# Layer 3's self-attention in one pass with three score buffers and shared output banks, and its cross-attention with plain head values

## The chip, the cores and the metric

One core of a Trainium2 chip runs the whole program. The metric is device time in microseconds of one execution, as the median of several. A profiled execution is longer by its profiler's share and is given beside its span, the time from its first to its last instruction.

## The reference

Four layers act on x (2 x 1024 tokens of 256 features) with a context of 2 x 64 tokens of 128 features. Each layer adds a gated attention part and a gated feed-forward part. The change touches layer 3's attention part only:

```
def mha(x, y, ..., causal):                 # H = 16 heads of D = 32
    q, k, v = ln(x) @ wq, ln(y) @ wk, ln(y) @ wv
    a = softmax(q @ k.T * D ** -0.5)        # over all keys
    if causal: a = a * (key > query)        # after the softmax: later keys only
    x_out = x + (a @ v, heads side by side) @ li1_w + li1_b
    return x_out + gelu(ln(x_out) @ li2_w + li2_b) @ li3_w + li3_b
x = ln(xx); x = x + mha(x, x, ..., causal=True)      # self-attention, 1024 keys
x = ln(x);  out = x + mha(x, ee, ..., causal=False)  # cross-attention, 64 keys
```

The softmax of the self-attention runs over all 1024 keys, but only keys after the query keep their weight. So a tile of 128 queries needs all its scores for the sum, and only the chunks of keys from its own on for the output.

## The kernel before

The program is a row of stages with a barrier between them. In each, every engine has its own list of instructions, written out by loops in Python, and engines wait for each other on semaphores that count. SP issues the DMAs, PE multiplies, ACT takes exponentials and copies, DVE reduces and copies, POOL multiplies and masks. PSUM has 8 banks of 512 fp32 columns.

`stage_self_project` normalises, multiplies by wq, wk and wv for pairs of 256 tokens, splits queries and keys into three bf16 parts and sends them to scratch in HBM, one entry for each batch and group of four heads (ENTRIES = 8). For the first batch it also sends the first group once more, as entry 8, a dummy. After the fourth pair SP waits until all that was sent has landed and loads entry 0 (`load_entry`: 16 DMAs of 256 KB and one of 512 KB), and then goes on with the sends of the next pairs. ACT waits for the sends of pair k-2 before it reuses their buffers (L2139).

`stage_self_attention` runs the entries in a hardware loop of two passes with a body of four entries (BODY = 4). After each pass the semaphores are cleared behind a barrier. An entry has 8 query tiles in the order 0, 7, 1, 6, 2, 5, 3, 4, and each tile four heads: 32 units. A block is one tile's four units; it has KC - si chunks of keys to turn and multiply, so 8, 1, 7, 2, 6, 3, 5, 4 in that order. In step v of the loop over units:

- PE computes the scores of unit v into one of two buffers of two banks (banks 0 to 3), once the exponentials of unit v-2 are taken. Then it transposes the masked probabilities of unit v-5 (`turn`), in groups of up to 4 chunks, into banks 4 and 5 in turn. From step 10 on it also does a quarter of the output product of a finished block (`output(w, q)`), into banks 6 and 7 in turn, one or two chunks at a time.
- DVE takes the row maxima of unit v (L2390), copies its share of the groups of unit v-5 (`store_turned`, side 1, L2361) and inverts the sum of unit v-1 (L2397).
- ACT copies its share (side 0), takes the exponentials of unit v with their sum (L2373), and every fourth step copies a finished output (L708).
- POOL multiplies by the inverse and masks.

Before an output begins, PE waits until the groups of that block are copied. They were transposed in the step before or earlier.

`stage_attention` serves layers 0, 2 and 3. It folds the keys into Wq, so that scores come straight from the features. For wider heads the values are folded into Wo as well (`fold_v`), and a tile's output is 8 products of 128 x 256. With `narrow`, which holds for layer 2 only (16 columns a head), the values stay as they are: the products of the probabilities with the head values go to bank 7, ACT copies them (`heads`, L708), and their product with Wo is the output. The norm's transposes use bank 7 too, so PE waits for that copy ahead of them, at every second tile.

Of the kernel before, what the change touches and what calls it, by code (L numbers as in the profile page):

```python
# [5 lines left out]
F32 = mybir.dt.float32  # L6
I32 = mybir.dt.int32
BF16 = mybir.dt.bfloat16
ALU = mybir.AluOpType
# [326 lines left out]
def stage_attention(core, a, name, width, scale, plan, following, source, out_tile, gate, bias,  # L336
# [16 lines left out]
    narrow = width * 4 <= KEYS  # L353
# [1617 lines left out]
def self_attention_scratch(nc):  # L1971


    def dram(name, shape, dtype):
        return nc.dram_tensor(name, shape, dtype, kind="Internal").ap()


    parts = [[dram(f"l3_{kind}_part{m}", [ENTRIES + 1, P, TOK], BF16) for m in range(3)] for kind in ("q", "k")]
    values = dram("l3_values", [ENTRIES + 1, P, KC, P], F32)
    heads_out = dram("l3_heads_out", [ENTRIES, P, TOK], F32)  # L1980
    return parts, values, heads_out
# [46 lines left out]
def stage_self_project(core, a, x1, scratch, entry, plan):  # L2028
# [6 lines left out]
    with ExitStack() as ctx:  # L2035
# [21 lines left out]
        with nc.Block() as block:  # L2057
            @block.sync
            def _(sp):
                total = [0, 0]  # L2060
                for k in range(PAIRS):
                    b, p, at = k // (PAIRS // B), k % 2, (k % (PAIRS // B)) * PAIR
                    places = [(b * GROUPS, GROUPS)]
                    if b == 0:
                        places.append((ENTRIES, 1))
# [23 lines left out]
            def sent_before(k):  # L2089

                return sum(16 * 8 * (2 if q < PAIRS // B else 1) for q in range(k % 2, k, 2))
# [104 lines left out]
def stage_self_attention(core, scratch, entry, following):  # L2196
# [8 lines left out]
    BODY = 4  # L2205
# [20 lines left out]
    assert BANKFULS % 2 == 0  # L2226

    def groups_through(u):

        return sum(1 for g in groups if g[0] <= u)  # L2230

    with ExitStack() as ctx:
# [13 lines left out]
        with nc.Fori(0, ENTRIES // BODY) as jj:  # L2246
            sem, clear_semaphores = named_semaphores(nc, "l3s")
            scores_ready, measured, exped, inverted = sem("scores_ready"), sem("measured"), sem("exped"), sem("inverted")
            masked, turned, stored = sem("masked"), sem("turned"), [sem("stored0"), sem("stored1")]
            out_ready, out_stored = sem("out_ready"), sem("out_stored")  # L2250
            out_sent = [sem(f"out_sent{e}") for e in range(BODY)]

            with nc.Block() as block:
                @block.sync
                def _(sp):
                    load_entry(sp, scratch, entry, BODY * jj + 1, 1)
                    for e in range(BODY):

                        sp.wait_ge(out_ready, KC * (e + 1))
                        if e < BODY - 1:  # L2260
                            load_entry(sp, scratch, entry, BODY * jj + e + 2, e % 2)
                        sp.wait_ge(out_stored, KC * (e + 1))
                        sp.dma_start(out_scratch[bass.ds(BODY * jj + e, 1)].rearrange("a p n -> p (a n)"),
                                     heads_out[:, e % 2, :]).then_inc(out_sent[e], 16)
                    for e in range(BODY):
                        sp.wait_ge(out_sent[e], 16)

                @block.gpsimd
                def _(pool):
                    for v in range(BODY * UNITS):  # L2270
                        si = tile_of(v)
                        pool.wait_ge(inverted, v + 1)
                        nc.gpsimd.tensor_tensor(ex[v % RING][:, si * P:], ex[v % RING][:, si * P:],  # L2273
                                                sm[:, v % RING:v % RING + 1].to_broadcast([P, TOK - si * P]), ALU.mult)
                        pool.drain()
                        nc.gpsimd.affine_select(out=ex[v % RING][:, si * P:(si + 1) * P], in_=ex[v % RING][:, si * P:(si + 1) * P],
                                                compare_op=ALU.is_gt, fill=0.0, base=0, pattern=[[1, P]],
                                                channel_multiplier=-1).then_inc(masked, 1)

                @block.tensor  # L2280
                def _(pe):
                    def ends_at(si):

                        return max(range(si, KC), key=lambda c: ((c - si) % R, c))

                    def scores(v):
                        p, si, r = v // UNITS % 2, tile_of(v), v % R
                        if v >= 2:
                            pe.wait_ge(exped, v - 1)
                        for h in range(2):  # L2290
                            for s in range(2):
                                last = nc.tensor.matmul(ps[:, 2 * (v % 2) + h, :],  # L2292
                                                        stack[p][0][s][:, r, si * P:(si + 1) * P],
                                                        stack[p][1][s][:, r, h * 512:(h + 1) * 512],
                                                        start=(s == 0), stop=(s == 1))
                        last.then_inc(scores_ready, 1)

                    def turn(v):
                        e, si = v // UNITS, tile_of(v)
                        pe.wait_ge(masked, v + 1)  # L2300
                        for g, (u, c0, size) in enumerate(groups):
                            if u != v % UNITS:
                                continue
# [424 lines left out]
```

## Time and profile before

| | us |
|---|---|
| median of 3 runs (2522.53 to 2523.38) | 2523.2 |
| the profiled execution | 2524.31 |
| its span | 2522.6 |
| PE busy | 2047.2 (81%) |
| DVE busy | 1367.6 (54%) |
| ACT busy | 929.6 (37%) |
| POOL busy | 710.5 (28%) |

The mean granted clock of TensorE is 0.902 of full speed. Busy shares are means over stages that differ: in the experts' stages PE is nearly alone, in the self-attention (about 969 to 1477 us) four engines work at once. So the stages are read one by one, from a table of stretches and from timelines.

### The profile page before, as it was taken

The numbers are of one execution on the slowest core, as the hardware profiler recorded it, in microseconds if no ns is written. First come the engines' busy times: TensorE is split into PE (matmuls) and PEld (weight loads), VectorE is DVE, ScalarE is ACT, GpSimd is POOL, SyncE is SP. The second block draws the span as 40 slices with busy tenths as digits, with TensorE's granted clock in tenths as the row PEclk, the third lists the DMA queues.
The fourth block names the chain that finished last, engine by engine and source line by source line (L and its number), as shares of the span: only waits on it lengthen the run. The fifth ranks groups of instructions, "written<-read, shape, count | busy, mean of one in ns | idle before, by whom it ended". The sixth has DMA issues, their size and how long they took to land. (4 is left out here: it accounts for less than half of the span.)

```text
span 2522.6 us, 36317 instructions
## 1 busy us (share of the span) xinstructions
PE 2047.2 (81%) x11904; PEld 1504.7 (60%) x11904; DVE 1367.6 (54%) x3511; ACT 929.6 (37%) x1859; POOL 710.5 (28%) x1199
## 2 busy tenths in 40 slices
PE   5983974467867677999799979969898589999991
PEld 4661863354444454555455558846687378888991
DVE  4871006535745765888688847757636432222332
ACT  4220321112324346888688843232232112222230
POOL 0223011030130125777577751102330230000005
PEclk9995995578979789999999989979999699999995
DMA  2004531000011286333333430110000525555684
GB/s 87 1 1 150 167 104 28 13 13 14 1 19 12 82 216 165 85 85 85 86 65 92 97 108 11 28 36 1 1 13 1 193 104 175 175 175 175 215 287 115
DMA packets 171504, 219.20 MB, mean 87 GB/s; under 512 B 39911, under 2 KB 133540, under 8 KB 165184
## 3 DMA queue, kind: packets, MB, share of 16 engines
q1 hardware_dynamic: 163344, 196.65, 26.7%
q0 software_dynamic: 7264, 20.31, 2.5%
q8 instruction: 88, 1.44, 0.2%
q14 instruction: 88, 0.72, 0.1%
q10 hardware_dynamic: 720, 0.07, 0.0%
HBM read 171.13 MB, written 46.14 MB: 86 GB/s over the span
## 5 line engine op out<-in xcount | busy, mean ns | idle before, releaser
L2390 DVE TENSOR_REDUCE l3s_mx<-banks 128x1 f32<-128x1024 f32 x256 | 313.1, 1223 | 96.7 <-PE banks L2292 93.8
L2292 PE MATMUL banks<-l_stack 128*128 128x512 bf16 x1024 | 268.1, 385 | 44.1 <-ACT xn_tokens L2373 21.0
L1012 PE MATMUL banks<-l3f_xrt,l3f_w 128*128 128x256 f32 (+1 forms) x1536 | 277.9, 342 | 2.7 <-issue 1.5
L1012 PEld LDWEIGHTS banks<-l3f_xrt,l3f_w 128*128 128x128 f32 x1536 | 249.6, 192 | 29.1 <-issue 3.3
L1302 DVE TENSOR_SCALAR l3f_sg<-banks 128x256 f32<-128x256 f32 (+1 forms) x192 | 72.0, 375 | 287.5 <-PE banks L1012 287.5
L2273 POOL TENSOR_TENSOR xn_tokens<-xn_tokens,l3s_sm 128x1024 f32<-128x1024 f32 (+3 forms) x128 | 201.6, 1575 | 50.3 <-DVE l3s_sm L2397 49.2
L222 PE MATMUL banks<-ident,xn_tokens 128*128 128x128 f32 x320 | 64.7, 338 | 166.8 <-DVE xn_tokens L211 148.0
L2292 PEld LDWEIGHTS banks<-l_stack 128*128 128x128 bf16 x1024 | 80.8, 98 | 163.3 <-ACT xn_tokens L2373 52.6
L2373 ACT ACTIVATE xn_tokens<-banks,l3s_mx 128x1024 f32<-128x1024 f32 x128 | 142.7, 1115 | 46.2 <-DVE l3s_mx L2390 45.1
L222 PEld LDWEIGHTS banks<-ident,xn_tokens 128*128 128x128 f32 x320 | 46.6, 172 | 188.4 <-DVE xn_tokens L211 133.0
L2373 ACT ACTIVATE x_features<-banks,l3s_mx 128x1024 f32<-128x1024 f32 x128 | 143.0, 1117 | 27.9 <-DVE l3s_mx L2390 27.6
L1077 ACT ACTIVATE l3f_sg<-l3f_sg 128x256 f32<-128x256 f32 (+1 forms) x192 | 72.2, 376 | 208.9 <-DVE l3f_sg L1302 208.9
L1025 PE MATMUL banks<-l3f_w,l3f_ht 128*128 128x256 f32 x624 | 138.5, 379 | 0.0
L930 POOL DMA_DIRECT2D l3f_results<-l3f_yt x24 | 15.8, 658 | 410.7 <-ACT l3f_yt L708 410.7
L1025 PEld LDWEIGHTS banks<-l3f_w,l3f_ht 128*128 128x128 f32 x624 | 116.8, 190 | 14.9
L2537 PE MATMUL banks<-x_features,weights 128*128 128x256 f32 x512 | 117.5, 390 | 4.3 <-ACT x_features L235 2.4
L2308 PEld LDWEIGHTS banks<-ident,xn_tokens 128*128 128x128 f32 x832 | 96.5, 140 | 29.1 <-issue 10.2
L2550 PE MATMUL banks<-weights,l3m_ht 128*128 128x256 f32 x512 | 113.2, 379 | 0.4 <-DVE l_x L2605 0.4
L2308 PE MATMUL banks<-ident,xn_tokens 128*128 128x128 f32 x832 | 112.6, 273 | 0.5 <-ACT l3s_pt L2359 0.5
L2537 PEld LDWEIGHTS banks<-x_features,weights 128*128 128x128 f32 x512 | 100.1, 196 | 19.5 <-issue 3.8
L2273 POOL TENSOR_TENSOR x_features<-x_features,l3s_sm 128x128 f32<-128x128 f32 (+3 forms) x128 | 92.4, 722 | 65.6 <-DVE l3s_sm L2397 64.6
L2359 ACT ACTIVATE l3s_pt<-banks 128x384 f32<-128x384 f32 (+2 forms) x192 | 97.0, 505 | 24.2 <-PE banks L2326 18.5
(532 smaller groups left out, 3925.4 us busy)
## 6 DMA issues: line engine op xcount, KB each, us to landing
l3f_w<-in_L_ffn_gate_up_w_dram SPq DMA_DIRECT2D x24, 2048.0 KB, 7.6
l3f_w<-in_L_ffn_down_w_dram SPq DMA_DIRECT2D x24, 1024.0 KB, 6.0
l_stack<-l_q_part SPq DMA_DIRECT2D x72, 256.0 KB, 6.0
l_stack<-l_k_part SPq DMA_DIRECT2D x72, 256.0 KB, 11.4
l0f_w<-in_L_ffn_W_dram SPq DMA_DIRECT2D x16, 1024.0 KB, 5.8
l_q_part<-l_stack SPq DMA_DIRECT2D x24, 256.0 KB, 3.0
l_k_part<-l_stack SPq DMA_DIRECT2D x24, 256.0 KB, 3.7
l3f_rows<-l3f_zero SPq DMA_DIRECT2D x13, 384.0 KB, 4.1
```

The costliest lines, as they stand in the source:

```text
L222: last = nc.tensor.transpose(ps[:, bank, c * PAIR + u * P:c * PAIR + (u + 1) * P], src(2 * j + u)[:, c * P:(c + 1) * P], core["ident"][:, :])
L1012: last = nc.tensor.matmul(ps[:, f % 4, h * PAIR:h * PAIR + size], w1_sb[:, p, dc, h * FF + f * P:h * FF + (f + 1) * P], xrt[:, p, dc, 0:si ...
L1025: last = nc.tensor.matmul(ps[:, 4 + p, u * D:(u + 1) * D], ht[:, p, f, u * P:(u + 1) * P], w2_sb[:, p, f, :], start=(f == 0), stop=(f == F ...
L1077: nc.scalar.activation(sg[:, f % 4, 0:size], sg[:, f % 4, 0:size], ACT.Silu).then_inc(silued, 1)
L2273: nc.gpsimd.tensor_tensor(ex[v % RING][:, si * P:], ex[v % RING][:, si * P:], sm[:, v % RING:v % RING + 1].to_broadcast([P, TOK - si * P]) ...
L2292: last = nc.tensor.matmul(ps[:, 2 * (v % 2) + h, :], stack[p][0][s][:, r, si * P:(si + 1) * P], stack[p][1][s][:, r, h * 512:(h + 1) * 512 ...
L2308: last = nc.tensor.transpose(ps[:, 4 + n % 2, c * P:(c + 1) * P], ex[v % RING][:, (si + c0 + c) * P:(si + c0 + c + 1) * P], core["ident"][ ...
L2359: last = op.activation(dst, src, ACT.Copy)
L2373: nc.scalar.activation(ex[v % RING][:, :], ps[:, 2 * (v % 2):2 * (v % 2) + 2, :].rearrange("p a n -> p (a n)"), ACT.Exp, bias=mx[:, v % RI ...
L2390: nc.vector.tensor_reduce(mx[:, v % RING:v % RING + 1], ps[:, 2 * (v % 2):2 * (v % 2) + 2, :].rearrange("p a n -> p (a n)"), AX_X, ALU.max ...
L2537: last = nc.tensor.matmul(ps[:, n % 4, 0:PAIR], w2[:, dc, f * P:(f + 1) * P], core["xt"][:, dc, PAIR * j:PAIR * (j + 1)], start=(dc == 0), ...
L2550: last = nc.tensor.matmul(ps[:, 4 + k % ring, u * D:(u + 1) * D], ht[:, k % 2, f, u * P:(u + 1) * P], w3[:, f, :], start=(f == 0), stop=(f ...
```

## The change

- Self-attention: the hardware loop goes; all 256 units are written out in one pass. There are three score buffers (banks 0 to 5), and scores wait for the exponentials of v-3. Turned probabilities and outputs share banks 6 and 7 in turn, in one running count of uses (`uses`), by whose parity ACT (even) or DVE (odd) copies them out. The output of a block is done at once, at one step in four, right after that step's transposes, and waits until every use before it is copied out on both sides. ACT and DVE copy an output at the start of their next step (`store_output`).
- The dummy entry goes, in scratch, in the projection's sends and as a load at the end.
- Cross-attention: `narrow` now holds for heads of 32 columns too, so layer 3's takes layer 2's path.

```diff
-    narrow = width * 4 <= KEYS
+    narrow = width * 2 <= KEYS
...
-                    if b == 0:
-                        places.append((ENTRIES, 1))
...
-    BODY = 4
+    SCORES = 3
+    uses = {}
+    for v in range(ENTRIES * UNITS + OUT):
+        if TURN <= v < ENTRIES * UNITS + TURN:
+            for g, group in enumerate(groups):
+                if group[0] == (v - TURN) % UNITS:
+                    uses["turn", (v - TURN) // UNITS, g] = len(uses)
+        if v >= OUT and (v - OUT) % R == 0:
+            uses["out", (v - OUT) // R] = len(uses)
+    def stored_through(side, n):
+        return (n + 2 - side) // 2
...
+                    if v >= SCORES:
+                        pe.wait_ge(exped, v - SCORES + 1)
...
+                        n = uses["turn", e, g]
+                        if n >= 2:
+                            pe.wait_ge(stored[n % 2], stored_through(n % 2, n - 2))
...
+                def output(w):
+                    e, si = w // KC, ORDER[w % KC]
+                    n = uses["out", w]
+                    for side in range(2):
+                        pe.wait_ge(stored[side], stored_through(side, n - 1))
+                    for c in range(si, KC):
+                        for r in range(R):
+                            last = nc.tensor.matmul(ps[r * W:(r + 1) * W, 6 + n % 2, 0:P], ...
+                    last.then_inc(out_ready, 1)
+                for v in range(ENTRIES * UNITS + OUT):
...
+                    if v < ENTRIES * UNITS:
+                        scores(v)
+                    if TURN <= v < ENTRIES * UNITS + TURN:
+                        turn(v - TURN)
+                    if v >= OUT and (v - OUT) % R == 0:
+                        output((v - OUT) // R)
...
+            def store_output(eng, op, v, side):
+                if v < OUT or (v - OUT) % R != 0:
+                    return
+                w = (v - OUT) // R
+                if uses["out", w] % 2 != side:
+                    return
+                eng.wait_ge(out_ready, w + 1)
...
+            @block.vector
+            def _(dve):
+                for v in range(ENTRIES * UNITS + OUT + 1):
+                    store_output(dve, nc.vector, v - 1, 1)
+                    if v < ENTRIES * UNITS:
+                        dve.wait_ge(scores_ready, v + 1)
+                        nc.vector.tensor_reduce(mx[:, v % RING:v % RING + 1], ...
+                    if v >= STORE:
+                        store_turned(dve, nc.vector, v - STORE, 1)
+                    if 1 <= v <= ENTRIES * UNITS:
+                        dve.wait_ge(exped, v)
+                        nc.vector.reciprocal(...).then_inc(inverted, 1)
...
-        nc.sync.wait_ge(loaded[0], 16 * LOADS * (ENTRIES // 2 + 1))
-        nc.all_engine_barrier()
```

## Rows read from the trace of the kernel before

**Rows 1.** Lines by shape, 940 to 1480 us: busy, mean ns, idle before.

```profile
L2390 DVE TENSOR_REDUCE l3s_mx<-banks 128x1 f32<-128x1024 f32 x256 | 313.1, 1223 | 96.7 <-PE banks L2292 93.8
...
L2361 DVE COPY l3s_pt<-banks 128x512 f32<-128x512 f32 x48 | 32.8, 682 | 6.3 <-PE banks L2308 5.7
...
L2361 DVE COPY l3s_pt<-banks 128x256 f32<-128x256 f32 x48 | 19.9, 415 | 0.9 <-PE banks L2308 0.9
```

**Rows 2.** Stretches: length; busy (count) of PE, PEld, DVE, ACT, POOL; PEclk, DMA, GB/s.

```profile
1089.29:1150.42 61.13, 58.92 (x562) 33.55 (x561) 51.91 (x88) 49.73 (x97) 45.74 (x65) 1.00 0.39 88
...
1209.68:1227.83 18.15, 8.90 (x119) 5.28 (x118) 3.59 (x8) 5.77 (x12) 3.82 (x6) 0.85 0.29 79
...
601.20:747.00 145.80, 114.08 (x608) 65.08 (x608) 100.12 (x145) 41.12 (x56) 23.58 (x112) 0.86 0.00 1
```

**Rows 3.** Timeline of units: start, length, engine, line, operation [idle before, releaser].

```profile
1089.29 1.23 DVE L2390 TENSOR_REDUCE l3s_mx<-banks 128x1 f32<-128x1024 f32 x1 [0.25 <-PE banks L2292]
...
1089.73 0.42 PE L2326 MATMUL banks<-l3s_pt,l_values_in 128*32 128x128 f32 x8
...
1090.09 1.04 PE L2292 MATMUL banks<-l_stack 128*128 128x512 bf16 x4
...
1090.43 0.41 DVE L2361 COPY l3s_pt<-banks 128x256 f32<-128x256 f32 x1
...
1090.96 0.60 PE L2308 MATMUL banks<-ident,x_features 128*128 128x128 f32 x4
...
1091.16 1.23 DVE L2390 TENSOR_REDUCE l3s_mx<-banks 128x1 f32<-128x1024 f32 x1 [0.24 <-PE banks L2292]
...
1093.21 0.64 PE L2326 MATMUL banks<-l3s_pt,l_values_in 128*32 128x128 f32 x16
...
1093.79 1.04 PE L2292 MATMUL banks<-l_stack 128*128 128x512 bf16 x4
```

**Rows 4.** Timeline: a copy on DVE and the weight load that waited for it.

```profile
1210.83 0.41 DVE L2361 COPY l3s_pt<-banks 128x256 f32<-128x256 f32 x1
...
1211.29 0.20 PEld L2308 LDWEIGHTS banks<-ident,xn_tokens 128*128 128x128 f32 x2 [0.21 <-DVE l3s_pt L2361]
```

**Rows 5.** Timeline: first and last reduction; a score group early in the second body.

```profile
968.92 1.22 DVE L2390 TENSOR_REDUCE l3s_mx<-banks 128x1 f32<-128x1024 f32 x1 [14.43 <-PE banks L2292]
...
1230.34 1.04 PE L2292 MATMUL banks<-l_stack 128*128 128x512 bf16 x4 [0.85 <-ACT xn_tokens L2373]
...
1468.58 1.23 DVE L2390 TENSOR_REDUCE l3s_mx<-banks 128x1 f32<-128x1024 f32 x1 [0.25 <-PE banks L2292]
```

**Rows 6.** Timeline of the projection: SP's issues and ACT's wait.

```profile
910.36 2.25 SPq L2078 DMA_DIRECT2D l_values<-l3p_vs  x4
...
914.27 1.78 SPq L2023 DMA_DIRECT2D l_stack<-l_q_part  x4
...
942.92 1.09 ACT L2139 ACTIVATE l_stack<-banks 128x512 bf16<-128x512 f32 x2 [9.00 <-DMA l_values<-l3p_vs]
```

**Rows 7.** Timeline of layer 3's cross-attention: folds, reductions, output.

```profile
1682.12 1.03 PE L482 MATMUL banks<-weights,l3a_blk 128*128 128x256 f32 x4
...
1773.58 1.22 DVE L631 TENSOR_REDUCE l3a_mx<-banks 128x16 f32<-128x1024 f32 x1 [0.98 <-PE banks L499]
...
1774.25 3.62 PE L542 MATMUL banks<-l3a_fold_v,l3a_pt 128*128 128x256 f32 x16
...
1781.78 1.23 DVE L631 TENSOR_REDUCE l3a_mx<-banks 128x16 f32<-128x1024 f32 x1 [1.11 <-PE banks L499]
```

**Rows 8.** Timeline of layer 2's cross-attention: scores, reduction, copy, transposes.

```profile
708.42 3.60 PE L499 MATMUL banks<-l2a_fold_q,x_features 128*128 128x512 f32 x8
...
712.35 1.21 DVE L631 TENSOR_REDUCE l2a_mx<-banks 128x16 f32<-128x1024 f32 x1
...
716.76 0.38 ACT L708 ACTIVATE l2a_heads<-banks 128x256 f32<-128x256 f32 x1
...
717.19 0.98 PE L222 MATMUL banks<-ident,xn_tokens 128*128 128x128 f32 x4 [2.66 <-ACT l2a_heads L708]
```

More of the change, by code:

```diff
@@ L1975, in dram @@
         return nc.dram_tensor(name, shape, dtype, kind="Internal").ap()
-    parts = [[dram(f"l3_{kind}_part{m}", [ENTRIES + 1, P, TOK], BF16) for m in range(3)] for kind in ("q", "k")]
-    values = dram("l3_values", [ENTRIES + 1, P, KC, P], F32)
+    parts = [[dram(f"l3_{kind}_part{m}", [ENTRIES, P, TOK], BF16) for m in range(3)] for kind in ("q", "k")]
+    values = dram("l3_values", [ENTRIES, P, KC, P], F32)
     heads_out = dram("l3_heads_out", [ENTRIES, P, TOK], F32)
@@ L2089, in sent_before @@
             def sent_before(k):
-                return sum(16 * 8 * (2 if q < PAIRS // B else 1) for q in range(k % 2, k, 2))
+                return sum(16 * 8 for q in range(k % 2, k, 2))
             @block.gpsimd
@@ L2349, in store_turned @@
                     for g, (u, c0, size) in enumerate(groups):
[L2350 to L2351 removed]
+                        if u != v % UNITS:
                             continue
[L2353 to L2357 removed]
@@ new lines, in turn @@
+                        last.then_inc(turned, 1)
+                def output(w):
+                    e, si = w // KC, ORDER[w % KC]
+                    n = uses["out", w]
+                    for side in range(2):
+                        pe.wait_ge(stored[side], stored_through(side, n - 1))
+                    for c in range(si, KC):
+                        for r in range(R):
+                            last = nc.tensor.matmul(ps[r * W:(r + 1) * W, 6 + n % 2, 0:P],
+                                                    values[:, e % 2, c, r * W:(r + 1) * W],
+                                                    pt[:, w % 2, r, c - si, :], start=(c == si),
+                                                    stop=(c == KC - 1))
+                    last.then_inc(out_ready, 1)
@@ new lines, in store_turned @@
+            def store_turned(eng, op, v, side):
+                if v >= ENTRIES * UNITS:
+                    return
+                e, w = v // UNITS, v // R
+                for g, (u, c0, size) in enumerate(groups):
+                    if u != v % UNITS or uses["turn", e, g] % 2 != side:
+                        continue
+                    n = BANKFULS * e + g
+                    eng.wait_ge(turned, n + 1)
+                    if w >= 2:
+                        eng.wait_ge(out_ready, w - 1)
+                    dst = pt[:, w % 2, v % R, c0:c0 + size, :].rearrange("p c n -> p (c n)")
+                    src = ps[:, 6 + side, 0:size * P]
+                    if side == 0:
+                        last = op.activation(dst, src, ACT.Copy)
+                    else:
+                        last = op.tensor_copy(dst, src)
+                    last.then_inc(stored[side], 1)
```

218 lines of the change are left out of this document (78 added, 140 removed).

## The prediction

> **What bounds the kernel now.** I read the page's slices first: the self-attention of layer 3 is the long even stretch from about 969 to 1477 us, a fifth of the span. The table of stretches then gives one entry (32 units of one tile and head) in its steady state: 61.13 us, in which PE is busy 58.92 and DVE 51.91 [rows 2]. So PE sets this stage, with DVE 9.2 us per entry behind it. The groups by line say the same: before the row maxima DVE stood idle 96.7 us, nearly all of it for PE's scores [rows 1]. Last I read the timeline of single units for the order on each engine, because the change is one of order. One step on PE: four score matmuls, 0.87 us until the transposes begin (1090.09 to 1090.96); the transposes, 0.11 us each plus 0.09 between parts; a piece of the output, 0.36 us for 8 records and 0.58 for 16, so 0.22 us per 8 records and about 0.13 fixed [rows 3]. On DVE: reduction, 1.14 us later the copy of turned probabilities, then the reciprocal [rows 3].
>
> From first to last reduction the stage takes 1468.58 - 968.92 = 499.7 us [rows 5]. That is 8 x 61.13 = 489.0, less one interval (1.9), plus the boundary between the two loop bodies, 18.15 where a step has 1.87 [rows 2], so 16.3; the sum, 503.4, is 3.8 too long, because the first entry of each body runs 1.9 faster (nothing to turn yet).
>
> **Self-attention, the boundary.** With one pass the drain and refill go: -16.3, and the second quick start with them: +1.9. Together -14.4 us. What is late next is the ordinary step.
>
> **Self-attention, the third score buffer.** Scores of unit v wait for the exponentials of v-3, not v-2. PE is busy 58.92 of 61.13 already, so this alone can give at most 2.2 us per entry. It also lets DVE work at its own rate wherever PE is ahead.
>
> **Self-attention, the outputs.** Before, the output of a block of four units goes in up to four pieces and waits for copies of transposes made at least one step earlier. Now turned probabilities and outputs share banks 6 and 7 in one running count n, and output n waits until everything up to n-1 is copied out on both sides. But n-1 is the group that PE transposed in this same step. I wrote the count out over one entry: in every block the second unit has a group on side 1, DVE's, whatever the block's length (for blocks of 1 to 4 chunks it is the only one, for 5 to 8 the first of two). DVE copies that group after the reduction of unit v. So once in four units PE must stand until DVE has finished the reduction of the newest scores and the copy; and no further scores can be issued meanwhile, since the output is ahead of them in PE's queue. Behind it wait scores v+1, on them DVE and ACT. The three buffers are empty at this point, by the order of the code.
>
> The hole that this leaves on DVE, from the end of the copy: 0.05 us to PE (copy ends 1211.24, PE's next load 1211.29 [rows 4]; I take 0.06), the output 0.13 + 0.22 m for m chunks, 1.07 from the scores' start to the reduction's [rows 3], less 0.15 for the reciprocal that fits in. That is 1.12 + 0.22 m. An entry has 8 outputs with m = 1 to 8, sum 36: 9.0 + 7.9 = 16.9 us. The output copies on DVE's side fall into the hole and cost nothing; without the hole they would be 4 x 0.28.
>
> DVE's own work: 51.9 us per entry. The sides change: of 24 copies per entry, two of 256 columns (415 ns) become two of 512 (682 ns) [rows 1], +0.5. So DVE's chain is 52.4 + 16.9 = 69.3 us per entry. Between outputs PE must keep up: for 8 chunks turned its step is 0.87 + 0.09 + 0.88 = 1.84, DVE's 1.14 + 0.60 + 0.12 = 1.86; equal, for short blocks PE is clearly quicker. Only for blocks of 5 and 7 does PE lag by 0.1 now and then; I add 0.3. Result 69.6 where 61.13 stood, though PE's own work falls (18 of the 26 pieces' fixed 0.13 go, 2.3 us).
>
> Bounds: if only PE's path counted (output, three steps, scores, reduction, copy) it would be 5.3 us fixed per output plus 0.22 m, 0.22 or 0.11 per turned chunk and the copy, 66.7 in all; if each of the 32 steps also lost 0.1 to a reciprocal or to POOL's queue, 73.
>
> In all: 8 x 69.6 = 556.8; the first entry lacks two outputs (4.2) and is 1.9 quicker; one interval less, 2.2: 548.5. Against 499.7: +48.8 us (with the bounds, +26 to +76). POOL (45.7 of 61.1 before) and ACT (49.7) stay below DVE. Drain and end of the stage stay as they are, within 1 us.
>
> **Projection.** The fifth copy of entry 0 goes: 8 DMA issues in each of the first four pairs, and the load of the dummy entry at the end. SP's issues take 2.25 us for 4 [rows 6], so 8 take 4.5. They sit right ahead of the wait for all sends, after which entry 0 is loaded (914.27). That load's 4.6 MB then hold up the sends, for which ACT waits 9 us until 942.92 [rows 6]. All of it moves up 4.5 us: -4.5 (none if the sends' bytes set it anyway, to -7 with 2 MB less to move). POOL's queue is not in it.
>
> **Cross-attention of layer 3.** It goes over to the path that layer 2 uses. Folds: 16 of 32 go, two records each of about 0.215 us at full clock, -6.9, and half the key/value products, about -0.9 [rows 7]; added are two value products of 512 columns (two records of 0.43 each, as in layer 2's scores [rows 8]), their mask on DVE (0.7, taken as a copy of 512 columns) and a handover: about -5.3. In the loop PE sets the time: 8.20 us from reduction to reduction with the norm's transposes, 7.76 without their four (0.44) [rows 7]. Of that 16 records of fold_v take 3.4; new are 8 records into Wo (1.8 with gaps) and 16 of 64-column weights. The latter no row shows. With 32 columns, four side by side, 8 records take 0.22 [rows 3], with 128 one takes 0.11: 16 records lie between 0.44 and 1.76. I take 0.88, half the array each, plus 0.14. A plain step becomes 7.24. At a norm step PE must now wait for ACT's copy of the head values, behind exp and the copy of the probabilities: in layer 2 that copy starts 4.41 us after the reduction and PE idles 2.66 for it, until 4.84 [rows 8]. Here it is 512 wide (0.6): transposes at 5.06, 0.5 for them, 3.44 scores, 0.2: 9.2 instead of 8.2. Twelve intervals: 95.4 before; 5.5 + 7 x 7.24 + 4 x 9.2 = 93.0 after, -2.4. The first of the twelve (5.5) is bound by DVE. The tail has one step more and its last outputs stand in the chain, twice at half clock: +3.5 to +5 by my estimate from the same records. Sum: -3 (from -6 to +12, if 64-column weights do not run side by side).
> By the page "TensorEngine Tiling (Array Packing)" of the Trainium skill (When to Use Tiling), weights of 64 columns give a column tiling of 2x; that is my 0.88. The trace before shows it for 32 columns only.
>
> **Sum.** +48.8 - 4.5 - 3 = +41. The profiled execution took 2524.31 us (span 2522.6), the median of the three is 2523.2; on the median: 2564.
>
> **The rivals.**
> *The output's wait is no more than the idle time DVE had* (faster). DVE idled 9.2 us per entry already; a third buffer can take that away. If the hole were 1.15 us per output instead of 2.1, an entry would stay at 61.1, and the rest decides: -14.4 - 4.5 - 3 = -22, 2501; with the waits met throughout, PE's work alone, about 58.5 per entry, 2480. It decides from 1.15 + 22/64 = 1.5 us per output. For it: PE's busy share; against it: output and scores alone are 1.07 + 0.13 + 0.22 m.
> *PE's clock falls* (slower still). In layer 2 a wait of 2.66 us is followed by matmuls at 1.2 GHz, and that stretch has a mean granted clock of 0.86; self-attention has 1.00 [rows 2, 8]. Here PE would wait 1.2 to 1.9 us per output. At half clock scores (0.87) and output (1.0) take about twice as long, 1.9 us more; at every second output that is 32 x 1.9, +60: 2625. In the first steps of a loop body PE waits 0.85 us of every 1.8 [rows 5] and the clock rises all the same, so I hold it unlikely.
> The Trainium skill ("TensorE: Matmul & The Clock Gate", A second HAM failure mode: psum-queue depth-cycling) says that short idle spells between groups, from cycling through PSUM banks, can make the clock swing and cost throughput; by it this rival would be the case.
> *Cross-attention's 64-column products run one after another*: 15 x 0.88, +13: 2577.
>
> **How the numbers follow.** Forecast 70% (own range 2540 to 2590), clock 10%, unpaired products 8%, the outputs' wait hidden 10% (of it 1 in 5 ends near no change), others 2%. Eight in ten: 2532 to 2594. Less than 0.2% (5 us) can't be told from no change. Faster 0.08, same 0.03, slower 0.89.
>
> **What would show it.** DVE's idle time before the reduction rises from 96.7 to some 140 us though the boundary is gone; before each output PE waits about 1.5 us, released by DVE's copy of turned probabilities; an entry takes 69 to 70 us; one gap of 18 us is missing; reductions in cross-attention 7.2 and 9.2 us apart. Wrong it is if outputs start less than 0.5 us after the transposes of their step, or if an entry stays below 62 us.

## The result, and the profile after

| | median us | runs | ratio to the kernel before (95%) |
|---|---|---|---|
| before | 2522.86 | 2519.68 to 2523.38 | |
| changed | 2558.07 | 2555.05 to 2561.02 | 1.0142 (1.0125 to 1.0160) |

The change makes the kernel 1.4% slower: 35 us, where the prediction had 41. The profiled execution took 2560.1 us, its span is 2558.5, so 35.9 more than the span before.

First the groups by line of the self-attention, 940 to 1520 us of the changed kernel (line, engine, operation, output<-input, shapes, count; busy us, mean ns; idle time of the engine before them, and what released it). They answer to [rows 1].

```profile
L2396 DVE TENSOR_REDUCE l3s_mx<-banks 128x1 f32<-128x1024 f32 x256 | 309.1, 1210 | 120.9 <-PE banks L2297 120.8
...
L2325 PE MATMUL banks<-l3s_pt,l_values_in 128*32 128x128 f32 x2304 | 76.2, 274 | 78.6 <-DVE l3s_pt L2359 72.9 <-ACT l3s_pt L2357 5.7
L2325 PEld LDWEIGHTS banks<-l3s_pt,l_values_in 128*32 128x32 f32 x2304 | 60.8, 109 | 92.9 <-issue 58.8 <-ACT l3s_pt L2357 34.0
...
L2359 DVE COPY l3s_pt<-banks 128x512 f32<-128x512 f32 x64 | 43.6, 681 | 3.5 <-PE banks L2313 3.5
...
L2374 DVE COPY weights<-banks 128x128 f32<-128x128 f32 x32 | 9.3, 291 | 28.8 <-PE banks L2325 28.8
```

DVE stood idle 120.9 us before the row maxima, where it was 96.7, though the 16 us of the boundary are gone. Almost all of it is a wait for PE's scores. PE in turn waited 72.9 us at the outputs (L2325) for DVE's copies of turned probabilities (L2359): 56 of the 64 waits. The other eight, one per entry, end with ACT's copy (5.7 us). Of the idle time of PEld, the weight load of the same outputs, 34.0 us end with ACT's copies (L2357). Before its copies of outputs (L2374) DVE stood another 28.8 us. The copy of 512 columns grew from 48 to 64 instances, as worked out.

One entry in the table of stretches, with the columns of [rows 2]:

```profile
1098.99:1167.55 68.56, 54.88 (x554) 35.73 (x560) 51.35 (x94) 48.51 (x93) 45.44 (x64) 1.00 0.34 78
```

The entry went from 61.13 to 68.56 us. PE was the full engine with 58.92 of 61.13; now it is busy 54.88 of 68.56 and no engine is full. When a stage gets longer while every engine in it gets emptier, a wait has taken over. The granted clock stays 1.00.

How it looks at one output, in the timeline of the changed kernel (start, length, engine, line, operation, [idle before, releaser]):

```profile
1118.66 1.21 DVE L2396 TENSOR_REDUCE l3s_mx<-banks 128x1 f32<-128x1024 f32 x1
...
1119.31 0.27 PE L2313 MATMUL banks<-ident,x_features 128*128 128x128 f32 x1
...
1119.78 0.15 DVE L2403 RECIPROCAL l3s_sm<-l3s_sm 128x1 f32<-128x1 f32 x1
1119.85 1.21 DVE L2396 TENSOR_REDUCE l3s_mx<-banks 128x1 f32<-128x1024 f32 x1
...
1120.97 0.28 DVE L2359 COPY l3s_pt<-banks 128x128 f32<-128x128 f32 x1
...
1121.40 1.95 PE L2325 MATMUL banks<-l3s_pt,l_values_in 128*32 128x128 f32 x64 [1.82 <-DVE l3s_pt L2359]
...
1123.51 0.81 PE L2297 MATMUL banks<-l_stack 128*128 128x512 bf16 x3 [0.16 <-issue]
...
1124.36 1.23 DVE L2396 TENSOR_REDUCE l3s_mx<-banks 128x1 f32<-128x1024 f32 x1 [3.04 <-PE banks L2297]
```

This is the output of an eight-chunk block; the group turned in its step has one chunk. DVE reduces the newest scores from 1119.85. PE put the one-chunk transpose into the queue ahead of the output, and it is long done. Its copy begins on DVE only at 1120.97, as the reduction ends. PE starts the output at 1121.40, having waited 1.82 us; the scores behind it start at 1123.51; DVE's next reduction comes at 1124.36, after 3.04 us of nothing to do. From the one reduction to the next it is 4.51 us where a step without an output takes 1.2 to 1.8.

First and last reduction of the stage (answers to [rows 5]):

```profile
967.22 1.23 DVE L2396 TENSOR_REDUCE l3s_mx<-banks 128x1 f32<-128x1024 f32 x1 [14.31 <-PE banks L2297]
...
1508.82 1.23 DVE L2396 TENSOR_REDUCE l3s_mx<-banks 128x1 f32<-128x1024 f32 x1 [0.66 <-PE banks L2297]
```

1508.82 - 967.22 = 541.6 us, 41.9 more than before, and no gap of 18 us stands between entries 4 and 5.

For the projection I take the two activation table loads that enclose it, of the kernel before and then of the changed one:

```profile
749.56 1.28 ACT L1938 ACT_TABLE_LOAD   x1
...
966.72 1.28 ACT L2373 ACT_TABLE_LOAD   x1 [10.58 <-PEq L44]
```

```profile
751.75 1.28 ACT L1938 ACT_TABLE_LOAD   x1
...
965.27 1.28 ACT L2387 ACT_TABLE_LOAD   x1 [10.73 <-PEq L44]
```

217.16 us became 213.52. Last, layer 3's cross-attention after the change: start of the stage, the first reduction, a step with the norm's transposes and the plain step behind it, and the last output of the tail (answers to [rows 7, 8]):

```profile
1701.10 0.10 POOL L424 MEMSET l3a_mask<- 128x4 f32 x1 [37.97 <-POOLq L44]
...
1722.18 1.22 DVE L631 TENSOR_REDUCE l3a_mx<-banks 128x16 f32<-128x1024 f32 x1 [3.79 <-PE banks L499]
...
1763.68 1.22 DVE L631 TENSOR_REDUCE l3a_mx<-banks 128x16 f32<-128x1024 f32 x1
...
1764.45 1.09 PE L522 MATMUL banks<-l3a_pt,l3a_v_blk 128*64 128x128 f32 x16
...
1765.47 1.99 PE L533 MATMUL banks<-weights,l3a_heads 128*128 128x256 f32 x8
...
1768.11 0.59 ACT L708 ACTIVATE l3a_heads<-banks 128x512 f32<-128x512 f32 x1
...
1768.75 0.66 PE L222 MATMUL banks<-ident,xn_tokens 128*128 128x128 f32 x4 [1.28 <-ACT l3a_heads L708]
...
1772.88 1.22 DVE L631 TENSOR_REDUCE l3a_mx<-banks 128x16 f32<-128x1024 f32 x1 [2.42 <-PE banks L499]
...
1780.13 1.22 DVE L631 TENSOR_REDUCE l3a_mx<-banks 128x16 f32<-128x1024 f32 x1 [1.00 <-PE banks L499]
...
1853.70 3.75 PE L533 MATMUL banks<-weights,l3a_heads 128*128 128x256 f32 x8 [2.96 <-DVE l_xo L657]
```

The stage starts with the mask at 1701.10 and reaches its first reduction 21.1 us later; before it was 26.5 (1660.83 to 1687.36). Reductions lie 9.20 us apart over a norm step (1763.68 to 1772.88) and 7.25 over a plain one (to 1780.13); before it was 8.20 and 7.76. The norm's transposes (L222) start 5.07 us after the reduction, released by ACT's copy of the head values, which began 4.43 after it.

**Where the 35.9 us are.** All from starts in the two timelines:

| stretch | before | after | difference | predicted |
|---|---|---|---|---|
| up to the projection's table load (nothing changed there) | 749.56 | 751.75 | +2.2 | 0 |
| projection, to the table load of the first exponential | 217.16 | 213.52 | -3.6 | -4.5 |
| from there to the first reduction | 2.20 | 1.95 | -0.2 | |
| self-attention, first to last reduction | 499.66 | 541.60 | +41.9 | +48.8 |
| its drain and the mlp, to the cross-attention's mask | 192.25 | 192.28 | 0 | 0 |
| cross-attention: prologue, loop, tail to the next table load | 172.87 | 168.77 | -4.1 (-5.4, -3.1, +4.4) | -3 (-5.3, -2.4, +3.5 to 5) |
| the rest | 688.9 | 688.6 | -0.3 | 0 |

The 2.2 us in front come from stages that both kernels share: over all kernels of this study, this start lies between 747.0 and 752.3. It also tells how small a difference of whole kernels can be believed.

### The profile page after: what moved, and what is told of

It is laid out like the page before. It is cut to its first block and busy times, and to the rows that moved or that the text cites. A ratio compares the mean times of both kernels' runs of the same rounds, so it can differ in the third digit from the quotient of the medians.

```text
span 2558.5 us, 36252 instructions
## 1 busy us (share of the span) xinstructions
PE 2003.5 (78%) x11932; PEld 1509.4 (59%) x11996; DVE 1361.6 (53%) x3538; ACT 919.1 (36%) x1826; POOL 706.6 (28%) x1202
## 5 line engine op out<-in xcount | busy, mean ns | idle before, releaser
L2396 DVE TENSOR_REDUCE l3s_mx<-banks 128x1 f32<-128x1024 f32 x256 | 309.1, 1210 | 120.9 <-PE banks L2297 120.8
L2297 PE MATMUL banks<-l_stack 128*128 128x512 bf16 x960 | 250.5, 381 | 21.3 <-PEq L44 12.2
L222 PE MATMUL banks<-ident,xn_tokens 128*128 128x128 f32 x320 | 65.2, 340 | 172.1 <-DVE xn_tokens L211 146.7
L222 PEld LDWEIGHTS banks<-ident,xn_tokens 128*128 128x128 f32 x320 | 46.2, 172 | 196.0 <-DVE xn_tokens L211 125.8
L2297 PEld LDWEIGHTS banks<-l_stack 128*128 128x128 bf16 x1024 | 95.1, 98 | 93.4 <-issue 24.2
L2313 PE MATMUL banks<-ident,xn_tokens 128*128 128x128 f32 x832 | 122.0, 277 | 21.6 <-DVE l3s_pt L2359 13.3
L2325 PE MATMUL banks<-l3s_pt,l_values_in 128*32 128x128 f32 x2304 | 76.2, 274 | 78.6 <-DVE l3s_pt L2359 72.9
L2325 PEld LDWEIGHTS banks<-l3s_pt,l_values_in 128*32 128x32 f32 x2304 | 60.8, 109 | 92.9 <-issue 58.8
```

Of the source, the lines that this page charges most:

```text
L222: last = nc.tensor.transpose(ps[:, bank, c * PAIR + u * P:c * PAIR + (u + 1) * P], src(2 * j + u)[:, c * P:(c + 1) * P], core["ident"][:, :])
L2297: last = nc.tensor.matmul(ps[:, 2 * (v % SCORES) + h, :], stack[p][0][s][:, r, si * P:(si + 1) * P], stack[p][1][s][:, r, h * 512:(h + 1) ...
L2313: last = nc.tensor.transpose(ps[:, 6 + n % 2, c * P:(c + 1) * P], ex[v % RING][:, (si + c0 + c) * P:(si + c0 + c + 1) * P], core["ident"][ ...
L2325: last = nc.tensor.matmul(ps[r * W:(r + 1) * W, 6 + n % 2, 0:P], values[:, e % 2, c, r * W:(r + 1) * W], pt[:, w % 2, r, c - si, :], start ...
L2396: nc.vector.tensor_reduce(mx[:, v % RING:v % RING + 1], ps[:, 2 * (v % SCORES):2 * (v % SCORES) + 2, :].rearrange("p a n -> p (a n)"), AX_ ...
```

## Experiments

The kernels of the experiments were timed beside fresh runs of the kernel before; its median was 2520.7 to 2522.8 us there, and each ratio is taken to those runs. Two theories stand against each other. A: the cost is the wait of each output for DVE's copy of the group turned in the same step, which stands behind the newest reduction. B: it is the output in one piece, or the sharing of banks, whatever is waited for. Entry times below are the distance from the first reduction of one entry to that of the next.

### The wait, at four of eight outputs

```diff
+ copied = max(uses["turn", e, g] for g, (u, _, _) in enumerate(groups) if u // R == w % KC)
  for side in range(2):
-     pe.wait_ge(stored[side], stored_through(side, n - 1))
+     pe.wait_ge(stored[side], stored_through(side, max(n - 2, copied)))
```

> The changed kernel, but output n waits only for what it reads and for its own bank: up to n-2, not n-1. Theory A (the hole is the wait for DVE's copy of the group turned in the same step, which stands behind the reduction): four of eight outputs per entry, those where the unit turned has 1 to 4 chunks, have only that copy as n-1 and lose the wait; the other four keep it, since n-2 is DVE's first group of the same step in the output's own bank. Their long intervals (4.51, 4.43, 4.34, 4.27 us from reduction to reduction) fall to about 3.0, what output and scores take on PE; the other four (3.4 to 4.0) stay. Entry 68.6 to 62 or 63 us, the kernel 2558 to about 2510 (2500 to 2525). Theory B (the output in one piece delays the scores, whatever it waits for): the long intervals stay over 4 us, kernel 2550 to 2560.

Measured: 2501.55 us (2497.66 to 2506.26), ratio to before 0.9923 (0.9904 to 0.9942). The entry is 61.66 us, by the starts of two entries:

```profile
1020.64 1.21 DVE L2397 TENSOR_REDUCE l3s_mx<-banks 128x1 f32<-128x1024 f32 x1
...
1082.30 1.20 DVE L2397 TENSOR_REDUCE l3s_mx<-banks 128x1 f32<-128x1024 f32 x1
```

The intervals at the outputs, the chunks of the output and of the unit turned beside them:

| output / turned | 5 / 4 | 4 / 8 | 8 / 1 | 1 / 7 | 7 / 2 | 2 / 6 | 6 / 3 | 3 / 5 |
|---|---|---|---|---|---|---|---|---|
| changed kernel | 4.28 | 4.04 | 4.51 | 3.38 | 4.43 | 3.46 | 4.33 | 3.69 |
| this kernel | 2.63 | 4.04 | 2.65 | 3.38 | 2.73 | 3.47 | 2.63 | 3.68 |

The four with a short turned block fell to 2.6 to 2.7 (I had said about 3.0), and the four others moved by 0.01 at most. The output in one piece is unchanged in all eight. That is theory A, output by output: the number in one wait costs the changed kernel 6.9 us per entry. Without it the kernel is 0.8% faster than before, although its entry still takes 0.5 us more; the boundary that is gone makes up for that.

### The output ahead of its step's transposes

```diff
  if v < ENTRIES * UNITS:
      scores(v)
+ if v >= OUT and (v - OUT) % R == 0:
+     output((v - OUT) // R)
  if TURN <= v < ENTRIES * UNITS + TURN:
      turn(v - TURN)
- if v >= OUT and (v - OUT) % R == 0:
-     output((v - OUT) // R)
```

The count `uses` changes its order in the same way, and the wait is that of the run above. ACT and DVE now copy an output in its own step, ACT first of all and DVE behind the reduction, not at the start of the next step.

> The changed kernel, but in its step the output goes ahead of the transposes (and in the running count too), and waits up to n-2: then all that it waits for was turned at least one step earlier. Theory A: no output waits for a copy that stands behind the reduction of its own step; the hole after the copy is gone at all eight outputs, and PE's own work sets the entry: 55 us busy and some gaps, 57 to 60 us instead of 68.6; the kernel 2465 to 2490, faster than both. Theory B (the one-piece output itself costs the time): intervals at outputs stay near 4 us, entry above 65, kernel above 2530.

Measured: 2485.09 us (2480.6 to 2486.64), ratio 0.9845 (0.9828 to 0.9863): 1.5% faster than before, 73 us faster than the changed kernel. The entry is 59.07 us (two of the six behind the first take 59.9 and 59.6). An output in its timeline:

```profile
1201.91 1.03 PE L2297 MATMUL banks<-l_stack 128*128 128x512 bf16 x4
...
1202.86 1.30 PE L2326 MATMUL banks<-l3s_pt,l_values_in 128*32 128x128 f32 x40
1202.97 1.23 DVE L2396 TENSOR_REDUCE l3s_mx<-banks 128x1 f32<-128x1024 f32 x1 [0.18 <-PE banks L2297]
...
1204.59 1.03 PE L2297 MATMUL banks<-l_stack 128*128 128x512 bf16 x4
...
1205.65 1.23 DVE L2396 TENSOR_REDUCE l3s_mx<-banks 128x1 f32<-128x1024 f32 x1 [1.06 <-PE banks L2297]
```

The output (L2326, 5 chunks) starts as the scores ahead of it end, and the reduction of these scores runs beside it. DVE's hole is still there, 1.06 us, but it is now that of the output's own length, not reduction plus copy plus output. Theory A's expectation is met, B's is not.

The same order with the old wait, up to n - 1, tells whether the place or the number matters:

> As the run with the output ahead of its step's transposes, but with the wait of the changed kernel, everything up to n-1. In the new count n-1 is always ACT's copy of the last group of the step before, which stands ahead of an exponential on ACT. Theory A (place in the queue decides, not how many uses back is asked for): entry 59 to 60 us, the kernel 2483 to 2495, as good as with n-2. Rival: asking for n-1 is itself dear; entry 62 to 66, kernel 2510 to 2540.

Measured: 2490.99 us (2487.17 to 2492.28), ratio 0.9865 (0.9850 to 0.9880), entry 59.71. The place in the queue, with the output's copies that move along with it, is worth 8.85 us per entry; the relaxed number is worth another 0.64. In the changed kernel's order the same relaxed number was worth 6.9.

### DVE's copy ahead of the reduction

```diff
+ copy_first = v >= OUT and (v - OUT) % R == 0
+ if copy_first:
+     store_turned(dve, nc.vector, v - STORE, 1)
  if v < ENTRIES * UNITS:
      dve.wait_ge(scores_ready, v + 1)
      ...
- if v >= STORE:
+ if v >= STORE and not copy_first:
      store_turned(dve, nc.vector, v - STORE, 1)
```

> The changed kernel, every wait and bank as it is, but in the steps with an output DVE copies its turned group ahead of the reduction. Theory A: the reduction (1.2 us) leaves PE's wait at all eight outputs; DVE now waits for the transposes of the step instead (0.1 + 0.11 per chunk, 1 to 4 chunks of its group, 0.4 on average), so about 0.8 us less per output, 6 per entry: 62 to 63 us instead of 68.6, the kernel about 2510 (2500 to 2525). Theory B (the wait isn't what costs): entry 68 to 70, kernel 2555 to 2570, since DVE only gets another wait.

Measured: 2520.39 us (2514.8 to 2523.21), ratio 0.9990 (0.9979 to 1.0000), entry 63.93. The kernel's time lies in theory A's range, the entry above its 62 to 63, and B's 2555 is excluded: with every wait and bank unchanged, the order of two instructions on DVE gives back 4.6 of the 7.4 us. The size was too hopeful. Taking each long interval with the one ahead of it, the outputs beside short turned blocks gained 0.70 to 1.12 us, those beside long ones 0.03 to 0.39: there n - 1 is ACT's second group, and in this run's trace ACT's copy ends all four of these waits. I had priced DVE's side alone.

### Two score buffers

```diff
-     SCORES = 3
+     SCORES = 2
```

> The changed kernel with two score buffers instead of three. Theory A: at each output all buffers run empty, and behind it PE must lead DVE again. Where short blocks are turned PE is quicker than DVE and the third buffer carries its lead into the next long block; without it PE waits for exponentials. Reductions 1.2 us apart in a row become 1.8. My estimate is 1 to 2 us more per block of four, entry 72 to 80, the kernel 2590 to 2650. Rival: the third buffer does nothing since the outputs empty all of them anyway; entry 68.6 to 69.5, the kernel 2558 to 2566.

Measured: 2609.2 us (2606.92 to 2611.68), ratio 1.0347 (1.0329 to 1.0364). Entries take 74.5 us, two of seven 77.7 and 76.2:

```profile
1032.51 1.21 DVE L2396 TENSOR_REDUCE l3s_mx<-banks 128x1 f32<-128x1024 f32 x1
...
1107.05 1.21 DVE L2396 TENSOR_REDUCE l3s_mx<-banks 128x1 f32<-128x1024 f32 x1
```

The long intervals stay as they are (4.28, 4.04, 4.53); of those between them, the ones of 1.19 us with three buffers become 1.7 to 2.2. The two longer entries have a cause of their own. In the table of stretches (columns of [rows 2]) the entry of 77.7 us, a stretch of 10 us within it and one of 3.5 us within that:

```profile
1107.05:1184.74 77.69, 60.20 (x562) 38.07 (x560) 52.41 (x95) 49.60 (x93) 45.72 (x64) 0.96 0.30 69
1127.00:1137.00 10.00, 7.70 (x84) 4.99 (x82) 4.93 (x10) 4.35 (x9) 4.74 (x7) 0.83 1.07 224
1131.00:1134.50 3.50, 3.21 (x61) 3.22 (x64) 0.21 (x2) 1.19 (x2) 2.23 (x3) 0.51 1.07 225
```

The granted clock was 1.00 up to 1131, then half of that, 1.2 GHz, for about 3.5 us (0.51 in that stretch), and PE's busy time rose from 57.0 us in the entry ahead to 60.2, with the same count of matmuls: 3.2 us, all that this entry is longer. Before it fell, PE had stood at each output as in the changed kernel, and between outputs it had waited for exponentials too (0.82 us at 1117.42, 0.64 us at 1128.65). That is what the prediction's second rival described, with 3.2 and 1.6 us in two entries where it had 60 us in all. That the waits made the clock fall is argued from this order of events and not shown. And with the output first:

> The run with the output ahead of its step's transposes (waits up to n-2), with two score buffers. It tells what the third buffer is worth once outputs don't wait. With the wait it was worth 6 to 9 us per entry (74.5 to 77.7 against 68.6). If the worth comes from refilling after a hole, it stays, since the hole of the output itself stays (intervals 2.7 to 3.2): entry 63 to 67, kernel 2515 to 2550. Rival, the prediction's bound for a PE-bound stage (at most 2.2 us per entry): entry 59 to 61.3, kernel 2485 to 2505.

Measured: 2538.94 us (2537.05 to 2540.93), ratio 1.0057 (1.0042 to 1.0073), entry 65.81 against 59.07. So the third buffer is worth 6.0 us per entry with the wait (where the clock holds) and 6.7 without. It does not fill the hole; it lets PE lead DVE again while short blocks are turned.

### The wait alone, in the kernel before

```diff
  if q == 0:
-     n = BANKFULS * e + groups_through(w % KC * R + R - 1)
+     t = min(w * R + OUT - TURN, BODY * UNITS - 1)
+     n = BANKFULS * (t // UNITS) + groups_through(t % UNITS)
```

> The kernel before, own banks for outputs and two score buffers, with one added wait: the first piece of each output waits for all copies of groups turned up to its own step, the wait that the change brings. Theory A (this wait is the cost): PE stands at each of eight outputs per entry for the reduction and DVE's copy, 1.2 + 0.3 to 0.7 us less what its transposes take; PE has 2.2 us of slack per entry, so an entry takes 68 to 72 us instead of 61.1, the kernel 2575 to 2605. Theory B (sharing of banks or one-piece outputs cost, not the wait): entry stays under 63, kernel 2520 to 2535.

Measured: 2602.21 us (2601.98 to 2603.16), ratio 1.0323 (1.0307 to 1.0339). The entry is 71.25 us:

```profile
1035.34 1.22 DVE L2391 TENSOR_REDUCE l3s_mx<-banks 128x1 f32<-128x1024 f32 x1 [0.24 <-PE banks L2292]
...
1106.58 1.22 DVE L2391 TENSOR_REDUCE l3s_mx<-banks 128x1 f32<-128x1024 f32 x1 [0.24 <-PE banks L2292]
```

Own banks, outputs in pieces, two buffers as before, and this wait alone costs 10.1 us per entry. With the runs above it is shown from both sides: taken out of the changed kernel the slowdown goes, put into the old one it comes.

### Outputs in one piece, in the kernel before

```diff
- chunks = [c for c in range(si, KC) if (c - si) % R == q]
+ chunks = list(range(si, KC)) if q == 0 else []
```

> The kernel before, with each output in one piece instead of up to four; banks and waits as before. Theory A: the piece count matters by its fixed cost on PE alone, 18 x 0.13 = 2.3 us less per entry; entry 59 to 61 us, kernel 2500 to 2520. Theory B (one-piece outputs starve DVE, with two score buffers above all): intervals of 3 us at long outputs not made up later, entry 63 to 67, kernel 2535 to 2570.

Measured: 2538.85 us (2537.39 to 2539.75), ratio 1.0071 (1.0056 to 1.0087), entry 62.6. The kernel's time lies in B's range of 2535 to 2570, near its lower end; the entry lies between the two theories, just below B's 63 to 67 and above A's 59 to 61. One piece costs 1.5 us per entry: PE's busy time falls by 3.2 us, but the intervals at long outputs (2.75 to 2.96 us) are not quite made up later. So B is a part of the truth, a seventh of the wait's size.

### One pass, and the fifth copy

The kernel before with `BODY = 8`:

> The kernel before with its self-attention loop over all eight entries in one body; banks, buffers, pieces and the fifth copy as before. By the prediction's term for the boundary: one interval of 18.15 us and one quick start go, -14.4 us in the stage, ratio 0.9943 (about 2506). Rival: the longer straight program costs more in instruction fetches than the boundary did, ratio 1.000 or above, and gaps on PE that no engine released.

Measured: 2506.41 us (2504.77 to 2510.54), ratio 0.9943 (0.9930 to 0.9957). First to last reduction 485.2 us, 14.4 less, the predicted term to a tenth. Then, in addition, without entry 0's second copy and its load:

> The kernel before with all entries in one body and, in addition, without the fifth copy of entry 0 and its load at the end: against the one-body kernel alone (2506.4 here) this is the projection's term. Prediction's term: -4.5 (0 to -7), 2502; the changed kernel's trace lost 3.6 us between the start of the stage before and the first exponential. Rival: the sends' bytes set the load's time anyway: no change, 2506, and the 3.6 us came from somewhere else.

Measured: 2505.73 us (2500.99 to 2508.01), ratio 0.9921 (0.9907 to 0.9934), so 0.0022 below the one-pass kernel, some 5 us with an uncertainty nearly as large. The traces settle it: from table load to table load the projection takes 216.8 to 217.2 us in the five profiled kernels that keep the copy and 213.4 to 214.2 in the nine without it. The term is 3.2 us between the two means, and 2.6 to 3.8 between single kernels.

### Cross-attention alone

The kernel before with `narrow = width * 2 <= KEYS`:

> The kernel before with the change to layer 3's cross-attention alone. By the prediction's terms: start of the stage to first reduction 26.5 to 21.2 us, steps 7.24 and 9.2 us apart instead of 7.76 and 8.20, the tail 3.5 to 5 longer, -3 in all: ratio 0.9988 (2520.7 to about 2517.5). Rival: products with 64-column weights run one after another, +13 us, ratio 1.005.

Measured: 2515.9 us (2512.9 to 2519.6), ratio 0.9980 (0.9970 to 0.9990). The interval takes in the 4.1 us (0.9984) of the two traces. The size is less sure than that figure looks: this run's own trace has 170.45 us for the stage, 2.4 less than before, and over all traces the stage takes 171.6 to 174.8 us with the old path and 166.6 to 170.5 with the new one. The sign holds in each, and the rival's +13 us (1.005) is out.

### Scores ahead of the output

The fastest kernel so far, and in a step with an output PE also issues the next unit's scores first:

```diff
+ out_step = v >= OUT and (v - OUT) % R == 0
- if v < ENTRIES * UNITS:
+ if v < ENTRIES * UNITS and not (v - 1 >= OUT and (v - 1 - OUT) % R == 0):
      scores(v)
+ if out_step and v + 1 < ENTRIES * UNITS:
+     scores(v + 1)
```

> The run with the output ahead of its step's transposes (waits up to n-2, three score buffers), and in the steps with an output PE also issues the next unit's scores ahead of the output, so that DVE has two units to reduce while the output runs. In that run PE is busy 56.3 of 59.5 us per entry, and outputs wait 2.2 us per entry for ACT's and 1.1 for DVE's copies (8.9 and 4.2 us in four and a half entries at most, of 17.8 and 8.5). Theory: the output now starts 0.9 us later, when these copies are done, so its waits go: entry 57 to 58.5, the kernel 2470 to 2480. Rival: PE's own work sets the entry already and the scores ahead wait for exponentials of three units back instead: entry 59 to 61, kernel 2485 to 2500.

Measured: 2483.66 us (2482.46 to 2486.24), ratio 0.9847 (0.9834 to 0.9860), entry 59.37 (59.07 without). No gain. (The waits quoted there were divided wrongly: 17.8 and 8.5 us stand over five entries, so 3.6 and 1.7 per entry.) They are indeed gone, and the time turned up elsewhere. From the list of waits over five entries (engine, tile, line <- releaser: us in total, times, longest), first what outputs waited for in the run without the scores ahead, then what scores waited for in the run with them:

```profile
PEld banks L2326 <- ACT l3s_pt L2358: 17.8, 20, 1.0
...
PE banks L2326 <- DVE l3s_pt L2360: 8.5, 20, 0.5
```

```profile
PEld banks L2297 <- ACT xn_tokens L2391: 9.2, 35, 0.4
...
PEld banks L2297 <- ACT x_features L2391: 4.6, 15, 0.4
```

The list of the run without the scores ahead has no wait of scores for an exponential; here there are 13.8 us of them (ACT's exponentials, L2391), since scores issued a step early find their buffer still unread. PE is busy 57.2 of 59.4 us, much as it was 58.9 of 61.1 before the change, so by that share PE's own work bounds the stage again.

## Why the prediction was right

**The mechanism** was right at each point it named: PE waits for a copy behind the newest reduction, once per four units; DVE then has nothing; no clock falls; the boundary goes. One wait in eight ends with ACT's copy and not with DVE's. DVE's idle time before the reductions rose to 120.9 us, not to some 140; with the 28.8 us before its output copies it is 149.7, so the idle time is there and in part stands ahead of another instruction. PE stood 1.6 to 1.8 us before outputs beside short turned blocks, and 0.7 to 0.9 beside long ones, whose transposes fill part of the time; I had said about 1.5 for all, with the line of refutation at 0.5. It sums to 9.9 us per entry.

**The hole.** By the prediction the next reduction comes 1.07 + 0.13 + 0.22 m + 0.06 after the copy's end. With the reduction (1.2) and the copy ahead of it, the eight-chunk output gives 1.2 + 0.28 + 1.26 + 1.76 = 4.50 (measured 4.51), the one-chunk output beside a seven-chunk block 1.2 + 0.68 + 1.26 + 0.22 = 3.36 (3.38), and the other six come out within 0.05 as well. This term carried the forecast, and it came from single rows of before.

**The entry** was 69.6 predicted, 68.56 measured, so eight entries were 8.3 us too high; the two ends of the stage, which I had made 1.4 us too short, bring that to the 6.9 us of the table. Within the entry two errors partly cancel. I put DVE's own work at 52.4 us; measured are 51.35 busy, and 1.16 of these are the four output copies that I had laid into the hole, so 50.2. Reductions became a little shorter (1210 ns, 1223 before, 0.4 per entry), and where steps follow each other closely, reductions start 1.19 us apart although reduction and reciprocal last 1.21 and 0.15: the records overlap, and I had added them. Against that DVE is idle 17.2 us beside those copies, 18.4 with them, where I had 16.9 and 0.3 for PE's lag, so 1.2 more: on long turned blocks the steps are 1.8 us, and PE falls behind more often than the 0.3 that I gave it.

**The third buffer.** "This alone can give at most 2.2 us per entry" is a bound for the kernel that it was said of, where no run tried a third buffer, and it is of no use for the one it was to go into. There it gives 6.0 us. The forecast did not suffer, because I built the new entry from its chain and not from the old one plus a saving, but the sentence hides what the change traded. By the runs, per entry: outputs in one piece +1.5 (61.1 to 62.6); shared banks with the output first, which no run took apart, +3.2 (65.8); third buffer -6.7 (59.1); output behind its transposes with the wait for n - 1, +9.5 (68.6). The design gains 2 us per entry; the place of one block in PE's program, with its wait for n-1, loses them nearly five times over.

**The boundary** -14.4 was measured as 14.4. **The projection** -4.5 was -3.6 in this trace and -3.2 over all traces. SP's timelines tell where it is. From the first send of the fourth pair to the last, SP takes 10.1 us before the change (902.52 to 912.61) and 5.9 after it (904.64 to 910.57): the eight issues are 4.2 us, near the 4.5 of the forecast. But SP then waits for the sends to land, 1.7 us before (until 914.27) and 2.9 after (until 913.44), and that takes 1.2 back. From the start of entry 0's load to the first exponential's table load it is 0.6 us less. The step that was too high is "all of it moves up 4.5 us". **Cross-attention** -3 was -4.1. Steps of 7.24 and 9.2 us were 7.25 and 9.20. The twelve intervals that I counted gained 1.8 us, not 2.4 (the first took 5.93, not 5.5), and the one ahead of them, which I had left alone, fell from 6.41 to 5.18. With the cross-attention changed alone these two are 5.53 and 6.39, so this last gain is not the change's in every kernel.

**The rivals.** *The wait hidden in DVE's idle time*: it was to decide at 1.5 us per output, and all of DVE's idle time, spread over the eight, is 17.2 / 8 = 2.15. It is what the kernel with the output first does, though: 2485, between the 2501 and the 2480 I gave. *PE's clock*: in the changed kernel the granted clock is 1.00 in every entry (0.99 in the first), with 64 waits of 0.7 to 1.8 us at the outputs. It was nearer than I thought: with two buffers it fell in two of eight entries, for 3.2 and 1.6 us. By the rule of the Trainium skill ("TensorE: Matmul & The Clock Gate", A second HAM failure mode: psum-queue depth-cycling) such idle spells between groups could have made the clock swing; the changed kernel's trace does not agree in this stage, the run with two buffers does in part. *64-column products one after another*: 16 of them take 1.02 us to the next line's start (1764.45 to 1765.47), where I had 0.88 + 0.14, half of the 0.11 that a 128-column one takes. By "TensorEngine Tiling (Array Packing)" (When to Use Tiling) of the Trainium skill it is a tiling of two; the trace agrees.

## What to carry to other kernels

When two streams of work are put into one count of banks, write the count out and look at what index n - 1 is, on which engine its copy stands, and behind what. A wait for something produced in the same step is a round trip through another engine's queue; moving the consumer ahead of the producer in the program (no wait removed) was worth 67 us here (2558 to 2491). A buffer's worth in a new design can't be read from the old kernel's slack: that slack was 2.2 us per entry here, and the third buffer gave 6.0 and 6.7 in designs that leave DVE without scores eight times per entry.

## What was not expected of the hardware

Row maxima of 1024 columns start 1.19 us apart in a row while each lasts 1.21 and a reciprocal of 0.15 lies between them: on DVE the records of neighbouring instructions overlap by some 0.1 us, and a sum of their lengths is that much too long per pair. And PE stood 0.7 to 1.8 us eight times per entry of 68.6 us, with no change of the granted clock; with two buffers and a few more waits between the outputs it fell twice. The layer 2 wait of 2.66 us stands in a stretch at 0.86 [rows 2, 8]. Which property of the waits makes the difference no run here tells.
